# Attention edges of a graph network: the destination rows are added by the transfer that gathers them

## What is computed

```python
s_n, v_n = _equiv_layernorm(s, v, gamma_s, beta_s, gamma_v)
msg_s = (s_n @ Ws_src)[src] + (s_n @ Ws_dst)[dst]
msg_v = einsum('ncx,cd->ndx', v_n, Wv_src)[src] + einsum('ncx,cd->ndx', v_n, Wv_dst)[dst]
m1_s, m1_v = _cg_tp(msg_s, msg_v, y0, y1, ...)      # tensor product with the edge's 4 numbers
a = ...(m1_s @ W_alpha)...                          # 4 attention logits per edge
val_s, val_v = ...(m1 @ W_val)...; h = second tensor product and maps   # 160 values per edge
```

## Time and profile before

| | before |
|---|---|
| median of three runs | 8251.5 us |
| profiled execution, span from first to last instruction (the page gives no other time of it) | 8256.1 us |
| busy over the span: PE / weight loads / DVE / ACT / POOL | 86% / 72% / 92% / 63% / 67% |
| in the stretch 1000 to 4000 us: PE / DVE / ACT / POOL | 91% / 99% / 67% / 73% |
| attention edges: first gather, last gather | 152.7 us, 4511.1 us |
| mean traffic over the span | 104 GB/s |

### The profile page before, as it was taken

The page is one execution under the profiler, slowest core; times in us unless marked ns, Lnnn a source line. Parts: engine busy times, 40 slices in busy tenths (PEclk is TensorE's granted clock), DMA queues, the critical chain, the costliest instruction groups (busy, mean ns, idle before and its releaser), DMA issues. The chain is left out here.

```text
span 8256.1 us, 202673 instructions
## 1 busy us (share of the span) xinstructions
PE 7100.0 (86%) x48227; PEld 5913.7 (72%) x48227; DVE 7559.8 (92%) x18614; ACT 5166.1 (63%) x17382; POOL 5566.3 (67%) x5953
## 2 busy tenths in 40 slices
PE   6999999999999999999999477779888888888888
PEld 4888888888888888888888366666555555555556
DVE  5999999999999999999999655554999999999999
ACT  2666666666666666666666311113777777777776
POOL 2777777777777777777776177771777777777773
PEclk5999999999999999999999699995999999999999
DMA  3443344334343444433343166651333333333332
GB/s 104 107 108 105 105 106 106 106 106 105 105 105 105 105 106 105 105 105 105 105 105 96 61 177 177 177 157 38 94 91 89 89 89 89 88 89 89 89 89 60
DMA packets 854751, 855.52 MB, mean 104 GB/s; under 512 B 478992, under 2 KB 636560, under 8 KB 854160
## 3 DMA queue, kind: packets, MB, share of 16 engines
q0 software_dynamic: 241920, 413.20, 20.5%
q1 hardware_dynamic: 612176, 437.39, 18.7%
q10 hardware_dynamic: 576, 4.01, 0.1%
HBM read 705.56 MB, written 148.44 MB: 103 GB/s over the span
## 5 line engine op out<-in xcount | busy, mean ns | idle before, releaser
L1219 POOL DMA_INDIRECT agg<-tab_conv,ce_idx x1808 | 1708.8, 945 | 866.0 <-issue 621.5
L464 POOL DMA_INDIRECT ae_gsrc<-tab_src,ae_idx x1616 | 1534.1, 949 | 751.8 <-issue 447.0
L467 POOL DMA_INDIRECT ae_gdst<-tab_dst,ae_idx x1616 | 1645.9, 1019 | 540.0 <-issue 538.2
L1308 PE MATMUL psum<-ce_prod,ce_plain 128*128 128x384 f32 x3616 | 1539.6, 507 | 328.3 <-DVE ce_prod L1281 275.5
L1293 ACT ACTIVATE ce_prod<-ce_raw,ce_y 128x64 f32<-128x64 f32 x5424 | 1464.0, 332 | 0.0
L1291 ACT ACTIVATE ce_prod<-ce_raw,ce_y 128x160 f32<-128x160 f32 x1808 | 752.6, 416 | 515.2 <-DVE ce_raw L1240 515.2
L709 ACT ACTIVATE ae_second_t<-psum 128x512 f32<-128x512 f32 x1212 | 731.7, 604 | 504.7 <-PE psum L619 499.0
L1310 PEld LDWEIGHTS psum<-ce_prod,ce_plain 128*128 128x128 f32 x3616 | 687.6, 190 | 479.4 <-issue 1.2
L1308 PEld LDWEIGHTS psum<-ce_prod,ce_plain 128*128 128x128 f32 x3616 | 547.0, 191 | 475.3 <-DVE ce_plain L1269 340.8
L627 PE MATMUL psum<-pack_sb,ae_first_t 128*128 128x200 f32 x3232 | 851.8, 345 | 2.2 <-ACT ae_first_t L705 2.0
L985 PE MATMUL psum<-ag_exval,ag_hot 128*128 128x164 f32 x3616 | 614.9, 314 | 237.2 <-issue 129.6
(11 more groups left out here) (215 smaller groups left out, 19257.6 us busy)
## 6 DMA issues: line engine op xcount, KB each, us to landing
ag_val<-h_dram SPq DMA_DIRECT2D x452, 320.0 KB, 3.2
h_dram<-ae_hout SPq DMA_DIRECT2D x404, 320.0 KB
agg<-in_query SPq DMA_DIRECT2D x452, 128.0 KB
ae_rin<-in_rin SPq DMA_DIRECT2D x404, 128.0 KB
agg<-tab_conv,ce_idx POOLq DMA_INDIRECT x1808
ae_gsrc<-tab_src,ae_idx POOLq DMA_INDIRECT x1616
ae_gdst<-tab_dst,ae_idx POOLq DMA_INDIRECT x1616
ag_idx<-in_eidx SPq DMA_DIRECT2D x452, 4.0 KB, 2.7
```

The lines of the kernel that those rows point to most:

```text
L464: pool.indirect_dma_start(gsrc[t.slot4][:, k, :], None, g["tab_src"], bass.IndirectOffsetOnAxis(ap=idx[t.slot4][:, k:k + 1], axis=0))\
L467: pool.indirect_dma_start(gdst[t.slot4][:, k, :], None, g["tab_dst"], bass.IndirectOffsetOnAxis(ap=idx[t.slot4][:, 4 + k:5 + k], axis=0))\
L1219: pool.indirect_dma_start(node[t.slot8][:, k, :], None, g["tab_conv"], bass.IndirectOffsetOnAxis(ap=idx[t.slot8][:, k:k + 1], axis=0))\
L1308: pe.matmul(b_a[t.slot], plain[t.slot4][:, k, :], prod[t.slot][:, k, 96:480], start=(k == 0), stop=False, skip_group_check=True)
```

## The change

The two rings `gsrc` and `gdst` and the single tile `msg` are replaced by one ring `msg` of four tiles. POOL first gathers the source rows of step m into `msg`, then waits for the source rows of step m - 1 (new semaphores `fetched`) and gathers the destination rows of step m - 1 onto them with `compute_op=ALU.add`. The addition on DVE and its semaphore `summed` are gone; the first products of DVE wait on `gathered` themselves, and POOL waits on `first_done`, which is counted when DVE has read the tile for the last time. SP's index load is one step less ahead and stands behind `y_early`. The loops of the stage are unrolled by four, as in the kernel before.

```diff
-        gsrc = [sb(f"gsrc{u}", [P, 4, C]) for u in range(4)]
-        gdst = [sb(f"gdst{u}", [P, 4, C]) for u in range(4)]
+        msg = [sb(f"msg{u}", [P, 4, C]) for u in range(4)]
...
-        msg = sb("msg", [P, 4, C])
...
+        fetched = [sem(f"fetched{u}") for u in range(2)]
...
-                    t = m + 6
-                    if t.inside(SUPER):
-                        wait(sp, gathered[t.slot4], 128 * t.quarter)
-                        sp.dma_start(idx[t.slot4][:, :], io["eidx"][t.n]).then_inc(idx_in[t.slot4], 16)
                     t = m + 2
...
+                    t = m + 5
+                    if t.inside(SUPER):
+                        wait(sp, gathered[t.slot4], 64 * t.quarter)
+                        sp.dma_start(idx[t.slot4][:, :], io["eidx"][t.n]).then_inc(idx_in[t.slot4], 16)
...
-                def body(t):
-                    pool.wait_ge(idx_in[t.slot4], 16 * (t.quarter + 1))
-                    wait(pool, summed, t.n - 3)
-                    pool.sem_inc(may_gather, 1)
-                    for k in range(4):
-                        pool.indirect_dma_start(gsrc[t.slot4][:, k, :], None, g["tab_src"], ...)\
-                            .then_inc(gathered[t.slot4], 16)
-                        pool.indirect_dma_start(gdst[t.slot4][:, k, :], None, g["tab_dst"], ...)\
-                            .then_inc(gathered[t.slot4], 16)
-                loop(pool, body, 0, SUPER, SUPER, 4)
+                def body(m):
+                    t = m
+                    if t.inside(SUPER):
+                        pool.wait_ge(idx_in[t.slot4], 16 * (t.quarter + 1))
+                        wait(pool, first_done, t.n - 3)
+                        pool.sem_inc(may_gather, 1)
+                        for k in range(4):
+                            pool.indirect_dma_start(msg[t.slot4][:, k, :], None, g["tab_src"], ...)\
+                                .then_inc(fetched[t.slot], 16)
+                    t = m + -1
+                    if t.inside(SUPER):
+                        pool.wait_ge(fetched[t.slot], 64 * (t.half + 1))
+                        pool.sem_inc(may_gather, 1)
+                        for k in range(4):
+                            pool.indirect_dma_start(msg[t.slot4][:, k, :], None, g["tab_dst"], ...,
+                                                    compute_op=ALU.add)\
+                                .then_inc(gathered[t.slot4], 16)
+                loop(pool, body, 0, SUPER + 1, SUPER, 4)
...
-                        dve.wait_ge(summed, t.n + 1)
+                        dve.wait_ge(gathered[t.slot4], 64 * (t.quarter + 1))
...
-                    t = m + 1
-                    if t.inside(SUPER):
-                        dve.wait_ge(gathered[t.slot4], 128 * (t.quarter + 1))
-                        wait(dve, first_done, t.n)
-                        wait(dve, outer_done, t.n)
-                        dve.tensor_tensor(msg[:, :, :], gsrc[t.slot4][:, :, :], gdst[t.slot4][:, :, :], ALU.add).then_inc(summed, 1)
```

More of the change, by code:

```diff
@@ L394, in attention_edges @@
             "idx_in", "early_in", "late_in", "rin_in", "gathered"))
+        fetched = [sem(f"fetched{u}") for u in range(2)]
         stored = [sem(f"stored{u}") for u in range(4)]
         filled, may_gather = sem("filled"), sem("may_gather")
-        ya_done, yb_done, yc_done, summed, spread, outer_done, cross_done, dot_done, first_done = (sem(x) for x in (
-            "ya_done", "yb_done", "yc_done", "summed", "spread", "outer_done", "cross_done", "dot_done", "first_done"))
+        ya_done, yb_done, yc_done, spread, outer_done, cross_done, dot_done, first_done = (sem(x) for x in (
+            "ya_done", "yb_done", "yc_done", "spread", "outer_done", "cross_done", "dot_done", "first_done"))
         gate_done, outer2_done, bent_done, rest_done, scored_done, logit_done, path2_done, values_done = (sem(x) for x in (
@@ L452, in body @@
                             .then_inc(stored[t.slot4], 16)
-                loop(sp, body, -6, SUPER + 5, SUPER, 4)
+                loop(sp, body, -5, SUPER + 5, SUPER, 4)
                 for u in range(4):
@@ L458, in _ @@
             def _(pool):
-                def body(t):
-                    pool.wait_ge(idx_in[t.slot4], 16 * (t.quarter + 1))
-                    wait(pool, summed, t.n - 3)
-                    pool.sem_inc(may_gather, 1)
-                    for k in range(4):
-                        pool.indirect_dma_start(gsrc[t.slot4][:, k, :], None, g["tab_src"],
-                                                bass.IndirectOffsetOnAxis(ap=idx[t.slot4][:, k:k + 1], axis=0))\
-                            .then_inc(gathered[t.slot4], 16)
-                        pool.indirect_dma_start(gdst[t.slot4][:, k, :], None, g["tab_dst"],
-                                                bass.IndirectOffsetOnAxis(ap=idx[t.slot4][:, 4 + k:5 + k], axis=0))\
-                            .then_inc(gathered[t.slot4], 16)
-                loop(pool, body, 0, SUPER, SUPER, 4)
+                def body(m):
[5 more added lines that the diff above has]
+                        for k in range(4):
+                            pool.indirect_dma_start(msg[t.slot4][:, k, :], None, g["tab_src"],
+                                                    bass.IndirectOffsetOnAxis(ap=idx[t.slot4][:, k:k + 1], axis=0))\
+                                .then_inc(fetched[t.slot], 16)
[4 more added lines that the diff above has]
+                        for k in range(4):
+                            pool.indirect_dma_start(msg[t.slot4][:, k, :], None, g["tab_dst"],
+                                                    bass.IndirectOffsetOnAxis(ap=idx[t.slot4][:, 4 + k:5 + k], axis=0),
+                                                    compute_op=ALU.add)\
+                                .then_inc(gathered[t.slot4], 16)
+                loop(pool, body, 0, SUPER + 1, SUPER, 4)
             @block.vector
@@ L486, in body @@
                     if t.inside(SUPER):
-                        v = comps(msg[:, :, CS:C])
-                        dve.wait_ge(summed, t.n + 1)
+                        v = comps(msg[t.slot4][:, :, CS:C])
+                        dve.wait_ge(gathered[t.slot4], 64 * (t.quarter + 1))
                         dve.wait_ge(ya_done, t.n + 1)
@@ L528, in body @@
                                           b_w[:, :, 0:P].rearrange("p k (a c) -> p k a c", a=2),
-                                          msg[:, :, 0:CS].unsqueeze(2).to_broadcast([P, 4, 2, CS]), ALU.mult)
+                                          msg[t.slot4][:, :, 0:CS].unsqueeze(2).to_broadcast([P, 4, 2, CS]), ALU.mult)
                         dve.tensor_tensor(comps(out[:, :, 256:352]), b_w[:, :, 192:224].unsqueeze(2).to_broadcast(three),
-                                          comps(msg[:, :, CS:C]), ALU.mult)
+                                          comps(msg[t.slot4][:, :, CS:C]), ALU.mult)
                         dve.wait_ge(cross_done, t.n + 1)
```

## The result

| | before | changed |
|---|---|---|
| median | 8252.35 us (8251.28 to 8258.34, 4 runs) | 8978.95 us (8974.77 to 8981.95, 4 runs) |
| ratio, 95% interval | | 1.0877 [1.0862, 1.0892]: slower |
| span of the profiled execution | 8256.1 us | 8977.1 us |
| last gather of the attention edges starts at | 4511.1 us | 5259.4 us |
| gathers of the convolution, first to last start | 5747.7 to 8141.2 us | 6465.8 to 8860.3 us |

The forecast was 8808 us, slower. The convolution's gathers start 718.1 us later and take 2394.5 us against 2393.5 us, so nearly all of the loss (721.0 us between the two spans) lies ahead of them. In the attention edges the adding gathers run from 161.8 to 5259.4 us: 5097.6 / 403 = 12.65 us a step, where it was 10.85.

What follows compares the result with a forecast made beforehand. DVE was taken to bound the kernel at 10.852 us a step, POOL 0.50 us behind. After the change POOL's 10.35 + 4 x 0.47 = 12.23 us, over 404 steps, adds 557 us: 8808 us, range 8030 to 9580.

Steps and rivals of the forecast that it cites:

- POOL the bound after the change: Attention edges: with four adding gathers POOL sets the step at 12.23 us, against 10.852 before.
- second behind DVE: Attention edges before the change: DVE sets the pace at 10.852 us a step, POOL follows 0.50 us behind.
- DVE's own step falls by 0.74 us: Removing the sum of messages on DVE shortens its own step from 10.852 to 10.11 us.
- POOL's floor of 10.35 us: POOL's unhindered step of eight plain gathers, taken as the middle of 10.26 and 10.43 us.
- x = 0.47 us, half of a plain gather: Extra POOL time per adding gather, between bounds 0 and 0.945 us; four a step.
- rival A: An adding gather costs POOL what a plain one does: 8050 us; chance 0.38, counted with a rival about PE.
- Break-even at x = 0.125 us: Extra time per adding gather at which four use up POOL's 0.50 us of room a step.
- The wait for fetched costs nothing: POOL's wait for the previous step's source rows costs 0; 2.7 us a step if the gathers were adjacent.
- Ring: Holding message tiles until DVE's last read delays no source gathers: cost 0.
- SP: Index load moved behind y_early, one step later: cost 0; if late, 2 to 3 us a step on POOL.
- DMA engines: Not a bound: if adding trebled the four gathers' time, the stage's share would go from 0.40 to about 0.65.
- the DMA share fall below 0.40: Expected sign in the attention edges if POOL sets the pace: DMA engines' share per time drops under 0.40.

Runs made afterwards that it cites:

- e1: Changed kernel with plain destination gathers in place of the adding ones, order, waits and ring kept: 7973.29 us, 0.9649 of before.
- e6: Changed kernel with the DVE sum put back as extra work on tiles of its own that nothing reads: 8989.04 us, 1.0889 of before.
- e2: Kernel before without its sum on DVE, which reads the source rows alone; both gathers stay: 7963.33 us, 0.9645 of before.
- e12: Kernel before without the three small copies of the edge numbers to PSUM, products reading the loaded tiles, on a third chip: 8924.27 us, 1.0805.
- e3: Changed kernel with one group of four by the adding gather, three by plain gathers and a shorter DVE sum: 8194.38 us, 0.9924 of before.
- e4: Changed kernel gathering 128, 96, 64 and 32 rows in its four groups; read for POOL's durations only: fourth gather 0.88 us plain, 1.34 adding.
- e7: Changed kernel without the lag of a step between source and adding gathers, on a slower second chip: 10972.45 us.
- e10: The kernel of e7 run once more, also on the second chip: 10950.29 us.

## Why the prediction held, point by point

- **POOL the bound after the change**: right. e1 (without the adding operand the loss is gone) and e6 (more work on DVE costs 10 us) show it, and POOL has no gap over 0.30 us. That POOL alone stood second behind DVE before the change is not shown: in e2 TensorE is full at 10.11 us as well. The prediction had 10.18 us for it.
- **DVE's own step falls by 0.74 us**: right. e1 and e2 reach 10.16 and 10.11 us, with DVE as full as before (2960.98 and 2965.52 us busy of 3000), and 10.11 was the forecast.
- **POOL's floor of 10.35 us**: the term that was too high, by 0.2 us. I had counted the lengthened gathers and the pauses of the earlier trace rows as POOL's own. The lengthened ones are collisions with DVE: by the count at e12, in the kernel before no gather is over 0.961 us without a DVE instruction with two inputs in SBUF in its first 0.3 us. Of the plain gathers between 1000 and 4000 us, 230 take over 1.1 us before, 134 in e1, 75 in e2 and 3 in e3, which keeps a sum of three groups. So POOL's time for a step depends on where DVE's instructions fall in its gathers, and the rows of one kernel do not give it for another. The longer pauses of the earlier trace rows were not traced to a cause.
- **x = 0.47 us, half of a plain gather**: mis-sized; it is 0.61. This is the term of the sum that carries most of the error. The reasoning behind it (half of the 0.945 us is per row and doubles) was wrong: e4 puts most of the extra into a fixed part. That the guess came near is luck of the bounds. The Trainium skill, "DMA: Bandwidth & Descriptors", section "Anatomy of one DMA", which spoke for rival A, calls descriptor generation small; by that x would have been about 0, and the trace with its 0.61 us does not agree.
- The two errors in the sum: 4 x 0.142 = +0.57 and -0.19 us, and 4 x 0.01 as the source gathers take 0.995 us here against 0.986 in e1. Together 0.42 us a step, 404 steps, 169 us: the distance from 8808 to 8979 us.
- **Break-even at x = 0.125 us**: with the floor of 10.16 it is (10.85 - 10.16) / 4 = 0.17 us for four adding gathers, and 0.69 us for a single one. That is why a quarter of the change pays (e3), which its expectation had excluded, and the whole does not.
- **The wait for fetched costs nothing**: right, but only thanks to the lag; without it POOL waits 3.1 us a step (e7, e10), where the prediction had 2.7 and the expectation of e7 1.4 to 2.0. An adding gather's own landing has a median of 3.6 us from its issue on the page of the profile.
- **Ring, SP, DMA engines**: no gap of POOL or wait of DVE goes back to them. The four gathers' engine time did not treble but about doubled. One sign was wrong: the prediction had the DMA share fall below 0.40, and it rose to 0.45, as each adding gather brings 96 packets more.
- **The clock**: PE's granted clock in the stretch fell from 1.00, its level of 2.4 GHz, to a mean of 0.91, so part of the stretch ran at 1.2 GHz. PE now waits for DVE up to 2.7 us at a time (L678, 337.8 us in all), where it was up to 0.8 (L677, 186.3 us). The clock was not in the forecast; as POOL waits for nobody in the stretch, it shows no cost.

## What to carry to other kernels

Moving an addition into an indirect transfer does not remove it: it moves it to the engine that issues the gathers, at 0.61 us for each list of 128 rows whatever their width, and still 0.46 us for 32 rows, against 0.19 us per group on DVE. Before such a move, get the issuing engine's floor by a kernel that simply leaves the addition out, and then move only as many groups as fill its room; here that was one of four, 8194 us. Take such a floor as one of that kernel, since DVE's instructions lengthen the gathers or not by where they fall. And a copy to PSUM that looks superfluous may be what keeps DVE's second operand out of SBUF, away from GpSimd's gathers.

## What the runs showed of the hardware

- An indirect DMA of 128 rows holds POOL for 0.945 us and an adding one for 1.557 us, with 0.30 us between them; 20 floats or 160 a row make no difference; 32 rows instead of 128 save 0.07 and 0.20 us.
- An adding gather makes 96 packets more than the 48 of a plain one, and twice the DMA engines' time.
- A DVE instruction with both inputs in SBUF that runs in a gather's first 0.3 us can lengthen it, in e12 up to 3.5 us in the stretch 1000 to 4000 us; without one no gather there took over 0.963 us. DVE itself is not slowed (0.542 us against 0.546).
- A dependent gather that waits for the one before it starts 4.4 us after it, where an independent one starts 1.25 us after it (e7).
